# The recurrence's given gates stored in the order in which a step reads them

## What is computed

```python
z = x_norm @ Wz + bz
gamma = jnp.clip(gamma_base * gamma_mod, 1e-06, 1.0 - 1e-06)

def step(h_prev, zt_gt):
    z_t, g_t = zt_gt
    gate = jax.nn.sigmoid(z_t @ Wgz + bgz + h_prev @ Wgh + bgh)
    h_tilde = (1.0 - gate) * h_prev + gate * z_t
    h_t = h_tilde + g_t * h_prev
    return (h_t, h_t)
_, h_seq_T = jax.lax.scan(step, h0, (z_T, gamma_T))
```

## Time and profile before

| what | value |
|---|---|
| median of 3 runs | 1553.15 us (1550.27 to 1555.27) |
| the profiled execution, its own time | 1554.73 us |
| its span in the profile | 1553.0 us |
| PE busy in the span | 1471.4 us (95%) |
| DVE, ACT, POOL busy | 767.8, 654.4, 262.8 us |
| granted TensorE clock over the span | 0.991 of full |
| the 100 steps of the recurrence | from 1111.8 to about 1370 us |

### The profile page before, as it was taken

How to read it: one execution, slowest core, us unless ns; L and a number is a source line. 1 busy time by engine, 2 the same in 40 slices (tenths; PEclk the granted TensorE clock), 3 DMA queues, 4 the chain that set the end, 5 groups by cost and what they waited for, 6 DMA issues and landing times.

```text
span 1553.0 us, 28673 instructions
## 1 busy us (share of the span) xinstructions
PE 1471.4 (95%) x12202; PEld 945.5 (61%) x12202; DVE 767.8 (49%) x1591; ACT 654.4 (42%) x1394; POOL 262.8 (17%) x443
## 2 busy tenths in 40 slices
PE   9888899999999999999999999999899999989998
PEld 8555565656655566555667765554566666655576
DVE  1676666766733256211233332324777777752132
ACT  3555555655635333111244432224554444442343
POOL 1433301010000010000022220000245444510000
PEclk9999999999999999999999999999999999999999
DMA  4311000000000020000200000000000000020032
GB/s 162 104 50 40 21 28 2 2 1 2 2 28 1 0 83 1 21 0 0 82 1 1 1 1 27 0 1 7 28 2 2 2 2 2 2 80 0 0 97 61
DMA packets 19562, 36.85 MB, mean 24 GB/s; under 512 B 2058, under 2 KB 17386, under 8 KB 18282
## 3 DMA queue, kind: packets, MB, share of 16 engines
q1 hardware_dynamic: 19434, 35.01, 6.8%
HBM read 33.36 MB, written 1.64 MB: 23 GB/s over the span
## 4 chain that ended last, share of the span: by engine, by line
PE 86%; DVE 7%; ACT 5%; issue 1%; DVEq 0%; ACTq 0%
PE psum L447 39%; PE psum L839 11%; PE psum L497 8%; PE psum L593 6%; PE psum L633 6%; ACT probs L1179 3%; PE psum L589 3%; DVE maxima L1527 2%; PE psum L532 2%; PE psum L944 2%; PE psum L972 1%; PE psum L953 1%; PE psum L937 1%; PE psum L985 1%; PE psum L627 1%
## 5 line engine op out<-in xcount | busy, mean ns | idle before, releaser
L1527 DVE TENSOR_REDUCE maxima<-psum 100x2 f32<-100x722 f32 (+3 forms) x332 | 245.5, 759 | 114.5 <-PE psum L532 93.9
L447 PE MATMUL psum<-x_resid,weights 128*128 128x400 f32 x832 | 293.7, 503 | 3.0 <-ACT probs L1179 1.7
L447 PEld LDWEIGHTS psum<-x_resid,weights 128*128 128x128 f32 x832 | 156.8, 191 | 120.1 <-issue 5.0
L1179 ACT ACTIVATE probs<-psum 128x800 f32<-128x800 f32 (+3 forms) x224 | 168.1, 787 | 100.1 <-PE psum L593 100.1
L839 PE MATMUL psum<-weights 128*128 128x400 f32 x512 | 174.8, 499 | 0.7 <-DVE maxima L1527 0.7
L447 PE MATMUL psum<-weights,ctx_t 128*128 128x256 f32 (+1 forms) x576 | 155.4, 393 | 1.3 <-DVE max_rows L1538 0.7
L839 PEld LDWEIGHTS psum<-weights 128*128 128x128 f32 x512 | 97.2, 190 | 75.1 <-DVE maxima L1527 0.8
L497 PE MATMUL psum<-ctx_t,weights 128*128 128x361 f32 x384 | 136.7, 481 | 2.1 <-DVE weights L1783 0.8
L1101 ACT ACTIVATE weights<-psum 128x400 f32<-128x400 f32 (+2 forms) x80 | 38.0, 476 | 205.4 <-PE psum L447 205.4
L447 PEld LDWEIGHTS psum<-weights,ctx_t 128*128 128x128 f32 (+1 forms) x576 | 99.1, 184 | 41.5 <-issue 9.5
L633 PE MATMUL psum<-probs,values 128*32 128x100 f32 (+5 forms) x3328 | 112.4, 253 | 2.8 <-ACT q_then_o L1101 1.8
(11 more groups left out here) (167 smaller groups left out, 2089.7 us busy)
## 6 DMA issues: line engine op xcount, KB each, us to landing
weights<-in_w SPq DMA_DIRECT2D x2, 3072.0 KB, 10.2
staged<-in_ctx SPq DMA_DIRECT2D x32, 128.0 KB, 2.1
values<-in_ctx SPq DMA_DIRECT2D x32, 128.0 KB, 2.2
weights<-in_w SPq DMA_DIRECT2D x3, 1024.0 KB, 5.1
weights<-in_src SPq DMA_DIRECT2D x1, 2368.0 KB, 13.8
weights<-in_w SPq DMA_DIRECT2D x1, 2048.0 KB, 7.9
weights<-in_tw SPq DMA_DIRECT2D x2, 1024.0 KB, 5.1
staged<-in_ctx SPq DMA_DIRECT2D x16, 105.0 KB, 2.3
```

Source lines behind the costliest of these rows:

```text
L447: i = nc.tensor.matmul(PS[0:rows, bk, 0:n], lhs, rhs, start=k == 0, stop=k == len(terms) - 1)
L1179: nc.scalar.activation(PT[0:kn, k % PROBS_KEPT, :, 0:n], PS[0:kn, bk:bk + 2, 0:n], ACT.Exp).then_inc(act_results, mark("act", f"{t} p{b} { ...
L1527: nc.vector.reduce_max(top, src, AX).then_inc(dve_results, mark("dve", f"{t} m{b} {j}"))
```

## The change

The tile GZP keeps its size and place. Before, it was ordered by half, part and column (batch, then time), so that the 96 values of one time lie 200 bytes apart and more. Now it is ordered by time, half, part and batch, so that the 96 values of one time are one run of 192 bytes. The product with the identity (L937) reads that run. Time is still the innermost dimension of the split, so its three instructions that write into GZP (L1843, L1846, L1850) now write elements that lie 192 bytes apart, and the three behind the cast (L1846, L1847, L1850) read a part back in that stride. No instruction is added, removed or moved on any engine: the order on each is the same, row for row.

```diff
-        GZP = region("gzp", DC * 3 * BS // 2).bitcast(BF16).rearrange("p (c r n) -> p c r n", c=DC, r=3)
+        GZP = region("gzp", DC * 3 * BS // 2).bitcast(BF16).rearrange("p (t c r b) -> p t c r b", t=S, c=DC, r=3)
...
-                given = GZP[:, :, :, :].rearrange("p c r (b t) -> p (c r) b t", b=B)[:, :, :, t]
+                given = GZP[:, t, :, :, :].rearrange("p c r b -> p (c r b)")
                 nc.tensor.matmul(PS[:, SCAN_BANK, 0:DC * 3 * B], IDB[:, :], given, start=True, stop=False)
...
-                gz, parts = T2[:, g % 2], GZP[:, :, :, cols(g)]
-                nc.vector.tensor_copy(parts[:, :, 0, :], gz).then_inc(dve_results, mark("dve", f"gz part0 {g}"))
+                gz = T2[:, g % 2].rearrange("p c (b t) -> p c b t", b=GB)
+                parts = GZP[:, :, :, :, g * GB:(g + 1) * GB].rearrange("p t c r b -> p c r b t")
+                nc.vector.tensor_copy(parts[:, :, 0], gz).then_inc(dve_results, mark("dve", f"gz part0 {g}"))
                 if due(f"gz part0 {g}"):
                     dve.wait_ge(dve_results, at(f"gz part0 {g}"))
-                nc.vector.tensor_tensor(parts[:, :, 1, :], gz, parts[:, :, 0, :], ALU.subtract).then_inc(dve_results, mark("dve", f"gz part1 {g}"))
-                nc.vector.tensor_tensor(gz, gz, parts[:, :, 0, :], ALU.subtract).then_inc(dve_results, mark("dve", f"gz rest {g}"))
+                nc.vector.tensor_tensor(parts[:, :, 1], gz, parts[:, :, 0], ALU.subtract).then_inc(dve_results, mark("dve", f"gz part1 {g}"))
+                nc.vector.tensor_tensor(gz, gz, parts[:, :, 0], ALU.subtract).then_inc(dve_results, mark("dve", f"gz rest {g}"))
                 if due(f"gz rest {g}"):
                     dve.wait_ge(dve_results, at(f"gz rest {g}"))
-                nc.vector.tensor_tensor(parts[:, :, 2, :], gz, parts[:, :, 1, :], ALU.subtract).then_inc(dve_results, mark("dve", f"gz split{g}"))
+                nc.vector.tensor_tensor(parts[:, :, 2], gz, parts[:, :, 1], ALU.subtract).then_inc(dve_results, mark("dve", f"gz split{g}"))
```

## The result

The changed kernel takes 1573.31 us (median of 4, 1572.29 to 1576.37) against 1553.27 us (median of 4): a ratio of 1.0132, interval 1.0115 to 1.015. It is 20 us slower (18 to 23 by the interval). The forecast was 1544, with 1540 to 1551 as its range. The part of the forecast that speaks of TensorE's read came out nearly as written; the split, whose growth it put at nothing, costs three times what the read gives.

The account below looks back on a forecast made before the run. TensorE was taken to bound the kernel, with the loop close behind in c2. From the 1553.15 us median, 9.3 us saved by the read and nothing lost in the split gave 1543.8, said as 1544; range 1540 to 1551.

Parts of the forecast that it names:

- The read: L937 in c2's steps: a contiguous read saves 0.118 us in each of 79 covered steps, 9.3 us.
- The loop: c2, from L944 through DVE, ACT and DVE to the next L944: 2.06 us, catching only one more step.
- The lower bound: c2: if the first L944's weight load must pass first, only 0.06 us a covered step is saved, 4.9 us.
- rival 3: c2: L937's slot shrinks only to the first load, or the loop catches up sooner; 4.9 us saved, 1548.3; chance 0.06.
- The room in gates: DVE's idle time around the split: 3.6 us for three groups' growth, 1.90 us for group 3 before L1855.
- PE is later by 3E - 3.6: Gates: TensorE's delay at the opening's maxima from three groups' split growth, for E over 1.33.
- late by E - 1.9: Gates, group 3: delay of the gamma products and first steps once the split's growth exceeds 1.90 us.
- E: Gates: growth per group of the split's four DVE instructions, in us; forecast as nothing.
- I take nothing, since the row of the same engine says so: Split on DVE: strided access adds no time, judged from L1871's PSUM read at 1.0 ns an element.
- The upper bound: Split on DVE at TensorE's stride price, 1.4 ns an element: E = 4.5, 9.9 + 2.6 = 12.5 us late.
- The prediction's other estimate: Split on DVE at GpSimd's half as much again for strided reads: E = 1.85, PE 1.95 us late, saving 7.3.
- first rival: Gates: 2-byte elements on separate lines slow the split and hold TensorE back; 1556, or 1569 at E = 7.7; chance 0.10.

Follow-up runs that it names:

- the read alone: Kernel before, with only the step's product reading a run of 96 values and the split writing as before: ratio 0.9952, median 1547.01 us.
- the dose between: Changed kernel's layout, but VectorE's split reads f32 400 bytes apart and writes runs of four: ratio 0.9978 to the kernel before, median 1550.61 us.
- the forms of TensorE's read above: Kernel before with ten forms of a 96-column bf16 product added at its end, 24 each: contiguous 0.042 us each, 16 bytes apart 0.171.

## Why the prediction was wrong

**The read** (right). 206 ns was forecast from L1017 and is what L937 takes; 0.118 us a covered step was forecast, and the distance went from 0.160 to 0.045. The steps' stretch is 8.9 us shorter, for 9.3. The loop catches a few more steps than it was said to: 25 have the longer distance, for 21, where one more was forecast. (The lower bound has a slip: 0.06 x 79 is 4.7 us, not 4.9, which moves rival 3 by 0.2 us.)

**The room in gates** (right but for its end). "PE is later by 3E - 3.6" and "late by E - 1.9" can be tested with the E that was measured. By durations the changed kernel's four instructions take 2.33, 4.157, 1.64 and 4.157 us, E = 12.28 - 3.70 = 8.6, which gives 22.1 + 6.7 = 28.8; 29.1 was measured, and in the dose between 2.4 for 2.0. The close total is luck in part, for it hides errors that cancel: L447 came 1116.64 - 1073.97 - 22.62 = 20.05 us late, not 22.1, and then the clock added 2.3 us on it; group 3 brought 6.7, but 0.8 of that is the clock again, on the products ahead of the first L937.

The error of 2 us isn't the rule's but comes from the overlap of durations. Taken from the cast to the instruction behind the split, the first three groups take 11.35, 11.98 and 11.33 us, for some 3.5, 3.45 and 4.2 before. They grew by 23.5, and 23.5 - 3.6 = 19.9 is within 0.2 of the 20.05 that L447 came late. For group 3 it is 1133.91 - 1122.57 = 11.34 us in the changed kernel, and in the kernel before 1107.95 - 1104.50 = 3.45, with this line behind the split:

```profile
1107.95 0.57 DVE L1538 TENSOR_TENSOR max_rows<-psum,constants 128x400 bf16<-128x400 f32 x1
```

The rule then gives 7.9 - 1.9 = 6.0, and the wait is 5.83. One thing was wrong with it: it put the wait at L1855 and the gamma products, and TensorE waits for L1538's rows of maxima, which stand ahead of them in the queue.

**The size of E** (the step that failed). "I take nothing, since the row of the same engine says so": the row was L1871, which reads PSUM, f32. The disputed thing was a write, into SBUF, of half-words. Three features differed, and it was taken as near because the engine was the same. The upper bound failed as well: TensorE's 1.4 ns an element was put on it as the dearest stride seen, but it is a price of reading too. The 2-byte write in strides costs 4.0 ns an element more than the contiguous one (3.17 / 800), and with E at 8.6 the term of nothing was 29 us. The prediction's other estimate, half as much again for a strided read, E = 1.85, fits VectorE's strided read (1.51 us for 0.99) and says nothing of the write. No row of the trace before showed a 2-byte write in strides, and the prediction said so under its first rival, with 2.4 ns as a mere "if", 1569 us and a chance of 0.05 for slower. The rival's mechanism and rule were right, and its place but for L1538: with E = 8.6 it gives 1553.15 - 9.3 + 28.8 = 1572.7, where 1573.31 was measured. It was the likeliest case that was wrong, and the range, which should have held the two ends of an unshown cost, left it out.

**The clock** (missing). That a wait of TensorE can be followed by the lower clock, and that the products behind it then pay again, has no term: 2.3 us in the changed kernel, 2.6 in the dose between, 1.7 behind c2 in most profiles with the quick read. In the profile of the read alone the clock costs 252.7 - 248.0 = 4.7 us in the steps and 1.7 behind them. Whether the median's 7.5 us for 9.3 is this clock isn't shown, since the interval, 4.8 to 10.1, holds both.

## What to carry to other kernels

Turning data has a price on one side or the other, and the sides aren't alike: a 2-byte write on a 16-byte line of its own took VectorE 4.0 ns an element more, a read in the same stride 0.65, and a strided read of PSUM cost ScalarE nothing. Here it paid to turn on an instruction that wasn't waited for, and to keep the innermost run at 8 bytes: such runs cost neither the writer nor TensorE anything, and the kernels in which ScalarE turns are 7 to 9 us faster than the kernel before. And where an edit's price isn't in the trace, the row to bound it by must match in direction, memory and element size before it matches in engine; if none does, the chance belongs on both sides. And before two rows are compared, look at the clock of each: half of the forms of TensorE's read above ran at half the clock.

## What was not expected

- VectorE writes 800 bf16 values 192 bytes apart in 4.16 us, f32 values in the same stride in 1.50, bf16 in runs of four in 0.99, the same as contiguous. The cast in runs of four keeps its fast form, 0.58 us; far apart it takes 2.17.
- ScalarE writing f32 16 bytes apart: 0.99 us for 400 elements, contiguous 0.59; reading PSUM 400 bytes apart: 0.60.
- TensorE's clock was at 0.50 in 1100 to 1120 us of the changed kernel, during its wait and behind it, and at 0.55 behind a wait of only 2 us in the dose between; 36 small products in that wait kept it at 1.00.
- Without any wait the clock fell to 0.50 while TensorE read columns 16 bytes apart, and the price of a line of 16 bytes stayed at 1.8 ns.
